# The last two groups turned on TensorE alone, and 4 of a second half's 16 moves handed from the sync queue to GpSimd

## The chip, the cores and the metric

One core of a Trainium2 chip runs the kernel. The metric is the device time of a whole execution, in microseconds (us), median over runs. The page and the trace come from one further execution taken with the hardware profiler.

## What is computed

One transformer block with adaptive layer norm, on x of 1 x 2048 x 128 in float32. Cut to what matters:

```python
h = _layernorm(x) * (1 + ca) + sa
q, k, v = split(einsum('bse,ehd->bshd', h, w_qkv), 3)        # 16 heads of 64
logits = einsum('bqhd,bkhd->bhqk', q, k) / sqrt(64)          # 2048 x 2048, causal
probs = softmax(where(mask, logits, neg))
x = x + ga * einsum('bshd,hde->bse', einsum('bhqk,bkhd->bqhd', probs, v), w_out)
h = _layernorm(x) * (1 + cb) + sb
expert = argmax(h @ Wr.T + br)                               # one of 8 for each token
x = x + gb * (relu(h @ W1[expert].T + b1[expert]) @ W2[expert].T + b2[expert])
```

## The kernel before

The 16 heads are taken as 8 pairs (PAIRS), and of each pair the 2048 queries as 8 groups of 256 (GROUPS). A group g has tiles_of(g) = 2g + 2 tiles of 128 keys. A group passes through these steps, each with the letter of its index in brackets (p pair, g group, r one of 4 rows of 128 queries of a head, j a key tile):

- score (L899, TensorE) puts scores into one of 4 PSUM banks; top (L1286, L1289, L1293, VectorE) copies them to `probs` in SBUF and takes the negated row maximum; exp (L1129, ScalarE) makes the exponentials in place, for one row r.
- The probabilities must be turned, keys to the partitions, before they can be multiplied by v. There are two ways. A *near* tile is turned on TensorE: turn (L912) is four 128 x 128 transposes into one of 3 PSUM banks, take (L1137 on ScalarE or L1322 on VectorE) copies them to one of 5 slots of `pT`. A *far* tile (j < far(g): 4 tiles of groups 3 and 4, 5 tiles of groups 5 to 7, none in groups 0 to 2) goes another way: shuffle (L1303, VectorE) transposes 32 x 32 blocks of a row r into `staged`, and moves (L650) carry the blocks to their partitions in `turned_far` by DMA.
- pv (L940, TensorE) multiplies a turned tile by v into one accumulating bank. Near tiles come first, far tiles last (pv_order, L66).
- sum, put and get (L1313, L699, L710) send reciprocal row sums through DRAM into a broadcast; norm (L1339), out (L953), add, and, in the last pair, back, resid, fresh, turn2, mod2, route, pick, rank, slots (L963 to L1415) finish 256 or 512 queries and find each token's place in a sorted list.

The moves. `staged` has two halves u: rows r = 0, 1 fill u = 0, rows r = 2, 3 fill u = 1. A half is 16 DMAs of 32 partitions each, in four batches a = 0 to 3 of four DMAs. The sync queue (SP) issues a = 0, 1 and GpSimd (POOL) a = 2, 3, of both halves; both queues run move_blocks (L641 to L651), which waits until the half is shuffled. Semaphores moved[u] (SP) and moved_soft[u] (POOL) each count 128 for a half. They are waited for in three places: by the far pv with j = 0 (L932, L933), for both halves; by the shuffle of the next group's rows r = 0 and r = 2 (L1301, L1302), for the same half, since `staged` is single; and by SP before the last stage (L731). There are 40 moves of a group (5 groups of 8 pairs).

SP also issues the puts (4 DMAs), the gets (2), the loads of each pair's weights, the blanks (L728), and in the last pair the 2 MB loads of W2 (L693) and W1 (L685) and b2 broadcast to all partitions (L686), each in a fixed place of its order. POOL also copies each chunk of k to its other 64 partitions (double, L795, two casts; the scores wait for it at L890) and, behind its last move, scatters the tokens (L803).

The order of every engine's work is made ahead, by class Plan (L101 to L413), a list scheduler on the host: it plays TensorE, ScalarE and VectorE with a duration per step (took, L318), a ready time per step (ready, L181), and moves that last 8 * ISSUE + LAND (5.2 + 4.2 us, move_at, L253). Each engine runs its list in that order with semaphore waits, so a change of a modelled time can reorder all three engines, SP (transfers, L280) and POOL (L159 to L162).

After the last pair: the experts' weights are transposed (wturn, L1036, L1039), the scattered tokens are read back in sorted tiles (L746), and 23 tiles go through the experts (L1055 to L1088).

Of the kernel before, what the change touches and what calls it, by code (L numbers as in the profile page):

```python
# [13 lines left out]
P = 128  # L14
# [4 lines left out]
PAIRS = 8  # L19
# [5 lines left out]
FAR_BUFS = 2  # L25
ISSUE = 650.0
LAND = 4200.0
# [33 lines left out]
def far(g):  # L61

    return FAR.get(g, 0)


def pv_order(g):  # L66

    return list(range(far(g), tiles_of(g))) + list(range(far(g)))
# [32 lines left out]
class Plan:  # L101
# [9 lines left out]
    def __init__(self):  # L111
        groups = [(p, g) for p in range(PAIRS) for g in range(GROUPS)]
        scores = [(p, g, r, c) for p, g in groups for r in range(4) for c in range(chunks(g))]
        turns = [(p, g, j) for p, g in groups for j in range(far(g), tiles_of(g))]
        pvs = [(p, g, j) for p, g in groups for j in pv_order(g)]
        self.moves = [(p, g) for p, g in groups if far(g)]
# [43 lines left out]
        for m, (p, g) in enumerate(self.moves):  # L160
            steps += [(self.move_at(m, u)[0] + 4 * ISSUE * i, "move", (p, g, u, 2 + i)) for u in range(2) for i in range(2)]
# [19 lines left out]
    def ready(self, kind, key):  # L181
# [8 lines left out]
        if kind == "pv":  # L190
            free = 0.0
            if key[2] == pv_order(g)[0] and p + g and min(groups_of(*self.part_of(p, g))) == g:
                free = at("norm", *self.part_of(*group_before(p, g)))
            return max(self.turned_at(key), at("value", p, key[2] // 4), free)
# [7 lines left out]
        if kind == "proj":  # L202

            last = (("score", p - 1, 2 * g + 1, 3, chunks(2 * g + 1) - 1), ("score", p - 1, GROUPS - 1, 3, g),
                    ("pv", p - 1, GROUPS - 1, max(range(4 * g, 4 * g + 4), key=pv_order(GROUPS - 1).index)))[key[2]]
            return max(self.ring_free(), at(*last) if p else 0.0)
        if kind == "top":
# [3 lines left out]
            if past and k0 < tiles_of(past[1]) * P:  # L211
                behind = at("shuffle", past[0], past[1], key[2]) if far(past[1]) else 0.0
                over = min((k0 + w) // P, tiles_of(past[1])) - 1
                if over >= far(past[1]):
# [9 lines left out]
        if kind == "norm":  # L224
            last = groups_of(p, g)[-1]
            i = p * CHUNKS + min(g, CHUNKS - 1) - 2
            return max([self.got(p, last), at("pv", p, last, pv_order(last)[-1])] +
# [9 lines left out]
        if kind == "wturn":  # L237
            free = max(at("pv", p, GROUPS - 1, pv_order(GROUPS - 1)[-1]),
# [14 lines left out]
    def move_at(self, m, u):  # L253

        if (m, u) not in self.moved:
            p, g = self.moves[m]
            begin = max(self.at("shuffle", p, g, 2 * u + r) for r in range(2))
            if m >= FAR_BUFS:
                q, f = self.moves[m - FAR_BUFS]
                begin = max(begin, self.at("pv", q, f, far(f) - 1))  # L260
            if u or m:
                begin = max(begin, self.move_at(m if u else m - 1, 1 - u)[0] + 8 * ISSUE)
            if begin >= NEVER:
                return NEVER, NEVER
            self.moved[m, u] = begin + HOP, begin + HOP + 8 * ISSUE + LAND
        return self.moved[m, u]

    def turned_at(self, key):

        p, g, j = key  # L270
        return self.move_at(self.move_no[p, g], 1)[1] if j < far(g) else self.at("take", *key)
# [8 lines left out]
    def transfers(self):  # L280
# [12 lines left out]
        for m, (p, g) in enumerate(self.moves):  # L293
            for u in range(2):
                for a in range(2):
# [4 lines left out]
                          self.at("shuffle", p, g - 1, 3) if far(g - 1) else 0.0) + HOP, "w2", (p,)))  # L300
# [17 lines left out]
    def took(self, kind, key, engine):  # L318
# [17 lines left out]
        if kind == "shuffle":  # L336
            return far(key[1]) * P / 0.96 + 100.0
# [43 lines left out]
    def choose_pe(self, now, soon):  # L381
# [11 lines left out]
        turn_at = place("turn", lambda k: (k[2] - far(k[1])) / float(tiles_of(k[1]) - far(k[1])))  # L393
# [23 lines left out]
def adaln_block(nc, x, w_qkv, w_out, Wr, br, W1, b1, W2, b2, c_in, wmod, out):  # L417
# [27 lines left out]
    with ExitStack() as ctx:  # L445
# [195 lines left out]
        def move_blocks(queue, key, landed):  # L641
# [4 lines left out]
            if m >= FAR_BUFS:  # L646
                q, f = plan.moves[m - FAR_BUFS]
                queue.wait_ge(pv_done, plan.order[q, f, far(f) - 1] + 1)
            for b in range(P // SQUARE):
                queue.dma_start(turned_far[b * SQUARE:(b + 1) * SQUARE, m % FAR_BUFS, u, a, 0:far(g), :],  # L650
                                staged[a * SQUARE:(a + 1) * SQUARE, u, b, 0:far(g), :]).then_inc(landed[u], 16)  # L651
# [4 lines left out]
        def _(sp):  # L656
# [21 lines left out]
            for s in plan.sp:  # L678
# [9 lines left out]
                elif s.kind == "w2":  # L688

                    sp.wait_ge(rows_turned, plan.number[p, GROUPS - 2, tiles_of(GROUPS - 2) - 1] + 1)  # L690
                    if far(GROUPS - 2):
# [38 lines left out]
            for u in range(2):  # L730
                sp.wait_ge(moved[u], 128 * len(plan.moves))  # L731
                sp.wait_ge(moved_soft[u], 128 * len(plan.moves))
# [107 lines left out]
        def _(pe):  # L840
# [26 lines left out]
            for s in plan.pe:  # L867
# [34 lines left out]
                elif s.kind == "turn":  # L902
# [3 lines left out]
                    if j == far(g):  # L906
# [8 lines left out]
                elif s.kind == "pv":  # L915
                    j = s.key[2]
                    first, last = pv_order(g)[0], pv_order(g)[-1]
# [10 lines left out]
                    if j < far(g):  # L928
# [251 lines left out]
        def _(dve):  # L1180
# [69 lines left out]
            for s in plan.dve:  # L1250
# [17 lines left out]
                elif s.kind == "top":  # L1268
# [6 lines left out]
                    if past and far(past[1]) and c == 0:  # L1275

                        dve.wait_ge(shuffled, 4 * plan.move_no[past] + r + 1)
                    if past and k0 < tiles_of(past[1]) * P and (r == 0 or (r == 2 and c == n - 1)):

                        over = min((k0 + w) // P, tiles_of(past[1])) - 1  # L1280
                        if over >= far(past[1]):
# [13 lines left out]
                elif s.kind == "shuffle":  # L1295
# [4 lines left out]
                    if m and h == 0:  # L1300
                        dve.wait_ge(moved[u], 128 * m)  # L1301
# [217 lines left out]
```

## Time and profile before

| | us |
|---|---|
| median of 3 runs | 979.15 |
| lowest, highest | 978.8, 984.84 |
| profiled execution, own time | 988.01 |
| its span, first to last instruction | 986.3 |
| TensorE busy in it | 913.3 |

The profiled execution is 8.86 us above the median of the runs. Engines: PE TensorE, PEld its weight loads, DVE VectorE, ACT ScalarE, POOL GpSimd; SPq the sync queue. Times of the trace are in us from the span's start. A pair lasts some 105 us.

### The profile page before, as it was taken

To read this page: it belongs to the slowest core of one execution; us is meant where nothing else is said; L and a number is where in the kernel's file an instruction comes from. 1 tells how busy PE (TensorE), PEld (TensorE's weight loads), DVE (VectorE), ACT (ScalarE), POOL (GpSimd) and SP (SyncE) were. 2 spreads that over 40 slices of the span, in tenths; PEclk is the share of its full clock that TensorE was granted. 3 is DMA by queue.
4 is the path that set the end of the run, shared out by engine and by line. 5 is a ranking of instruction groups with operands and counts; after the bars stand their busy time and mean duration, and the time that the engine had idled before them with its cause. 6 is when DMAs were issued, how large, how long until landed. Compare 5 with 4: busy or idle time off the path is not lost.

```text
span 986.3 us, 19842 instructions
## 1 busy us (share of the span) xinstructions
PE 913.3 (93%) x6115; PEld 674.7 (68%) x6115; DVE 761.9 (77%) x2426; ACT 633.8 (64%) x1158; POOL 422.6 (43%) x765
## 2 busy tenths in 40 slices
PE   4999999989998999899998999899989999995796
PEld 3776767667675767677676767676767666773796
DVE  6898869875997769785988599867978689971463
ACT  4876668656774768665865677577857566551574
POOL 0274515442364316542554236431745144445054
PEclk9899999999999999999999999999999999986898
DMA  2035312342144302531245214430343013372120
GB/s 81 12 91 133 100 38 64 104 125 66 29 111 109 92 23 79 136 99 47 56 106 131 66 30 113 111 95 22 88 118 87 20 47 84 87 226 69 31 67 18
DMA packets 107211, 79.13 MB, mean 80 GB/s; under 512 B 32935, under 2 KB 94163, under 8 KB 107106
## 3 DMA queue, kind: packets, MB, share of 16 engines
q1 hardware_dynamic: 85378, 51.57, 19.7%
q0 software_dynamic: 21728, 26.29, 10.2%
q8 instruction: 50, 0.82, 0.4%
q14 instruction: 55, 0.45, 0.2%
HBM read 18.21 MB, written 11.77 MB: 30 GB/s over the span
## 4 chain that ended last, share of the span: by engine, by line
PE 59%; SPq 16%; DVE 12%; issue 5%; DMA 4%; ACT 2%; another core or an unknown queue 1%; POOL 1%; POOLq 0%; DVEq 0%; ACTq 0%
PE ps L940 18%; PE ps L899 13%; SPq L650 12%; PE ps L912 12%; PE ps L878 4%; DVE probs L1286 4%; DMA turned_far<-staged 3%; PE ps L882 3%; PE ps L1064 2%; DVE probs L1289 2%; PE ps L1075 2%; PE ps L953 2%; SPq L710 2%; SPq L699 2%; DVE staged L1303 1%
## 5 line engine op out<-in xcount | busy, mean ns | idle before, releaser
L650 POOL DMA_DIRECT2D turned_far<-staged x640 | 313.1, 497 | 353.4 <-DVE staged L1303 340.4
L1129 ACT ACTIVATE probs<-probs,neg_max 128x128 f32<-128x128 f32 (+15 forms) x256 | 308.7, 1207 | 151.2 <-DVE neg_max L1293 148.6
L899 PE MATMUL ps<-k_both,q_both 128*128 128x512 f32 (+2 forms) x1280 | 344.1, 393 | 12.9 <-DVE probs L1286 7.7
L899 PEld LDWEIGHTS ps<-k_both,q_both 128*128 128x128 f32 x1280 | 208.7, 190 | 84.9 <-issue 30.5
L1286 DVE TENSOR_SCALAR_CACHE_REDUCE probs<-ps 128x512 f32<-128x512 f32 (+1 forms) x384 | 243.4, 662 | 5.0 <-PE ps L899 4.0
L1137 ACT COPY pT<-ps 128x512 f32<-128x512 f32 (+1 forms) x341 | 177.1, 557 | 94.8 <-PE ps L912 76.3
L912 PE MATMUL ps<-ident,probs 128*128 128x128 f32 x1440 | 203.8, 278 | 2.3 <-ACT probs L1129 1.4
L912 PEld LDWEIGHTS ps<-ident,probs 128*128 128x128 f32 x1440 | 172.4, 143 | 46.5 <-issue 23.3
L940 PE MATMUL ps<-pT,v_sb 128*64 128x256 f32 (+1 forms) x1568 | 179.1, 370 | 5.7 <-DVE pT L1322 3.8
L940 PEld LDWEIGHTS ps<-pT,v_sb 128*64 128x64 f32 x1568 | 104.4, 137 | 74.0 <-issue 19.1
L1303 DVE STREAM_TRANSPOSE staged<-probs 128x640 f32<-128x640 f32 (+1 forms) x160 | 122.0, 778 | 37.6 <-DMA turned_far<-staged 15.9
L1289 DVE CUSTOM_DVE_ANT_0 probs<-ps,causal 128x256 f32<-128x256 f32 (+3 forms) x256 | 130.2, 509 | 8.1 <-PE ps L899 7.8
L795 POOL CAST k_both<-k_both 64x1024 fp32r<-64x1024 f32 x64 | 66.4, 1037 | 148.2 <-DVE k_both L1265 145.6
L940 PE MATMUL ps<-turned_far,v_sb 128*64 128x256 f32 x736 | 93.0, 400 | 17.8 <-DMA turned_far<-staged 17.8
L940 PEld LDWEIGHTS ps<-turned_far,v_sb 128*64 128x64 f32 x736 | 56.1, 143 | 43.0 <-issue 24.3
L878 PE MATMUL ps<-hT,w_pair 128*128 128x512 f32 x128 | 63.4, 599 | 0.2 <-DVE q_both L1261 0.2
L1261 DVE SCALAR_TENSOR_TENSOR q_both<-ps,q_both 64x512 fp32r<-64x512 f32 x64 | 44.1, 689 | 20.9 <-ACT q_both L1115 19.7
L1322 DVE COPY pT<-ps 128x512 f32<-128x512 f32 (+1 forms) x51 | 31.5, 617 | 30.0 <-PE ps L912 15.1
L1339 DVE TENSOR_TENSOR oT<-ps,rinv_b 128x512 f32<-128x512 f32 (+1 forms) x33 | 22.1, 670 | 41.7 <-PE ps L940 40.7
L1129 ACT ACTIVATION_READ_ACCUMULATOR probs<-probs,neg_max 128x1 f32 x256 | 48.8, 190 | 0.0
L1265 DVE TENSOR_TENSOR k_both<-ps,k_both 64x512 fp32r<-64x512 f32 x64 | 44.1, 689 | 5.7 <-ACT k_both L1115 4.5
L1293 DVE TENSOR_REDUCE neg_max<-row_max 128x1 f32<-128x1 f32 (+3 forms) x256 | 39.8, 155 | 8.9
(147 smaller groups left out, 700.7 us busy)
## 6 DMA issues: line engine op xcount, KB each, us to landing
turned_far<-staged POOLq DMA_DIRECT2D x384, 40.0 KB, 2.5
turned_far<-staged SPq DMA_DIRECT2D x384, 40.0 KB, 2.0
x_sorted<-blank SPq DMA_DIRECT2D x19, 458.5 KB, 5.3
rinv_b<-spread_rows SPq DMA_DIRECT2D x128, 64.0 KB, 2.7
turned_far<-staged SPq DMA_DIRECT2D x256, 32.0 KB, 1.9
turned_far<-staged POOLq DMA_DIRECT2D x256, 32.0 KB, 1.8
spread_rows<-rinv_rows SPq DMA_DIRECT2D x256, 0.5 KB
probs<-in_L_ffn_W_dram SPq DMA_DIRECT2D x1, 2048.0 KB, 11.6
```

The costliest lines, as they stand in the source:

```text
L650: queue.dma_start(turned_far[b * SQUARE:(b + 1) * SQUARE, m % FAR_BUFS, u, a, 0:far(g), :], staged[a * SQUARE:(a + 1) * SQUARE, u, b, 0:fa ...
L795: nc.gpsimd.tensor_copy(k_split[h][own_half(1 - h), :, cols], k_split[h][own_half(h), :, cols]).then_inc(k_doubled[c], 1)
L878: pe.matmul(ps_ring[:, s.bank, :], w_pair[:, p % 2, j, :], hT[:, c * BANK:(c + 1) * BANK], start=True, stop=True).then_inc(bank_full[s.ban ...
L899: m = pe.matmul(ps_ring[:, s.bank, 0:w], q_split[r % 2][:, q0:q0 + P], k_split[r % 2][:, part, k0:k0 + w], start=(part == 0), stop=(part = ...
L912: m = pe.transpose(ps_turn[:, n % TURN_BANKS, P * r:P * r + P], probs[g % 2][:, r, j * P:j * P + P], ident[:])
L940: m = pe.matmul(ps_o[D * h:D * h + D, o_half + P * u0:o_half + QG], v_sb[:, j, D * h:D * h + D], of_head[:, h], start=(j == first), stop=( ...
L1129: act.activation(row, row, ACT.Exp, bias=neg_max[:, g, r:r + 1], accum_out=row_sum[:, g, r:r + 1]).then_inc(exp_done, 1)
L1137: act.copy(pT[:, n % PT_SLOTS, lo:BANK], ps_turn[:, n % TURN_BANKS, lo:BANK]).then_inc(turn_taken[n % TURN_BANKS], 1)
L1261: m = dve.scalar_tensor_tensor(out=q_split[h][own_half(1 - h), cols], in0=whole, scalar=Q_SCALE, in1=q_split[h][own_half(h), cols].bitcast ...
L1286: dve.tensor_scalar(row, ps_ring[:, bank, 0:w], 1.0, LOWEST, ALU.mult, ALU.max, accum_out=highest).then_inc(bank_free[bank], 1)
L1289: dve.tensor_tensor_reduce(row, ps_ring[:, bank, 0:w], causal[:, BANK - w:], 1.0, LOWEST, ALU.add, ALU.max, highest).then_inc(bank_free[ba ...
L1303: dve.transpose(staged[:, u, :, 0:far(g), h * SQUARE:(h + 1) * SQUARE], probs[g % 2][:, r, 0:far(g) * P].rearrange("p (j b i) -> p b j i", ...
```

## The change

Three things: the far tiles are dropped for the last two groups of the last pair (groups 6 and 7 of pair 7), so that all their tiles are turned on TensorE; of a second half (u = 1) SP issues only batch a = 0 and POOL a = 1, 2, 3, while a first half stays two and two; and the planner's times for a half become 8 * ISSUE = 5.2 us for u = 0 and 12 * SOFT_ISSUE = 6.0 us for u = 1. The functions far and pv_order take the pair too; the calls that only pass it on are left out.

```diff
+LAST_NEAR = 2
+HARD, SOFT = (128, 64), (128, 192)
 ISSUE = 650.0
+SOFT_ISSUE = 500.0
...
-def far(g):
-
-    return FAR.get(g, 0)
+def far(p, g):
+
+    return FAR.get(g, 0) if p * GROUPS + g < PAIRS * GROUPS - LAST_NEAR else 0
...
-            steps += [(self.move_at(m, u)[0] + 4 * ISSUE * i, "move", (p, g, u, 2 + i)) for u in range(2) for i in range(2)]
+            steps += [(self.move_at(m, u)[0] + 4 * SOFT_ISSUE * i, "move", (p, g, u, 2 - u + i)) for u in range(2) for i in range(2 + u)]
...
             if u or m:
-                begin = max(begin, self.move_at(m if u else m - 1, 1 - u)[0] + 8 * ISSUE)
+                begin = max(begin, self.move_at(m if u else m - 1, 1 - u)[0] + (12 * SOFT_ISSUE, 8 * ISSUE)[u])
...
-            self.moved[m, u] = begin + HOP, begin + HOP + 8 * ISSUE + LAND
+            self.moved[m, u] = begin + HOP, begin + HOP + (8 * ISSUE, 12 * SOFT_ISSUE)[u] + LAND
...
             for u in range(2):
-                for a in range(2):
+                for a in range(2 - u):
                     steps.append((self.move_at(m, u)[0] + 4 * ISSUE * a, "move", (p, g, u, a)))
...
                         if j == 0:
                             for u in range(2):
-                                pe.wait_ge(moved[u], 128 * m_no + 128)
-                                pe.wait_ge(moved_soft[u], 128 * m_no + 128)
+                                pe.wait_ge(moved[u], HARD[u] * (m_no + 1))
+                                pe.wait_ge(moved_soft[u], SOFT[u] * (m_no + 1))
...
                     if m and h == 0:
-                        dve.wait_ge(moved[u], 128 * m)
-                        dve.wait_ge(moved_soft[u], 128 * m)
+                        dve.wait_ge(moved[u], HARD[u] * m)
+                        dve.wait_ge(moved_soft[u], SOFT[u] * m)
```

## Rows read from the trace of the kernel before

**Rows 1.** Busy time by stretch: us, busy per engine, granted clock, DMA share, GB/s.

```profile
50.00:785.00 735.00, 707.91 (x4756) 509.92 (x4755) 592.10 (x1782) 497.27 (x869) 331.25 (x616) 1.00 0.32 83
785.00:889.40 104.40, 98.39 (x635) 72.40 (x634) 91.30 (x347) 60.52 (x95) 45.48 (x87) 0.95 0.39 110
889.40:909.60 20.20, 10.09 (x45) 5.85 (x46) 2.51 (x11) 1.42 (x3) 10.56 (x12) 0.61 0.20 56
...
313.00:317.00 4.00, 4.00 (x21) 2.41 (x18) 2.26 (x7) 0.00 (x0) 1.58 (x4) 0.57 0.28 74
```

**Rows 2.** Waits, 50 to 785 us: total us, times, longest.

```profile
PE ps L940 <- DMA turned_far<-staged: 17.5, 12, 3.5
PE ps L899 <- DVE probs L1286: 6.5, 7, 1.0
...
DVE staged L1303 <- DMA turned_far<-staged: 15.9, 9, 2.7
```

**Rows 3.** Timeline of SP, 296 to 316.5 us.

```profile
299.51 1.49 SPq L699 DMA_DIRECT2D spread_rows<-rinv_rows  x4
302.49 1.29 SPq L710 DMA_DIRECT2D rinv_b<-spread_rows  x2
...
304.52 11.37 SPq L650 DMA_DIRECT2D turned_far<-staged  x16
```

**Rows 4.** Timeline of POOL, 255 to 366 us.

```profile
269.47 2.15 POOL L795 CAST k_both<-k_both 64x1024 fp32r<-64x1024 f32 x2
...
298.92 3.91 POOL L650 DMA_DIRECT2D turned_far<-staged  x8 [6.44 <-DVE staged L1303]
```

**Rows 5.** Timelines of PE from 204 and 311 us, of DVE from 307 us.

```profile
204.08 4.07 PE L940 MATMUL ps<-turned_far,v_sb 128*64 128x256 f32 x20 [3.11 <-DMA turned_far<-staged]
...
312.63 0.84 DVE L1303 STREAM_TRANSPOSE staged<-probs 128x640 f32<-128x640 f32 x1 [3.10 <-issue]
...
312.80 4.00 PE L940 MATMUL ps<-turned_far,v_sb 128*64 128x256 f32 x20 [3.46 <-DMA turned_far<-staged]
```

**Rows 6.** The chain that ended last: pieces of TensorE at full clock.

```profile
335.84 1.92 PE ps L912 x16
...
419.86 2.37 PE ps L940 x20
```

**Rows 7.** Issues of line L650, 150 to 785 us: ns min/median/max.

```profile
L650 SPq DMA_DIRECT2D turned_far<-staged x480: 512/591/1766, 157.0 to 765.2; - x160
L650 POOL DMA_DIRECT2D turned_far<-staged x480: 496/496/505, 157.2 to 761.5; - x160
```

**Rows 8.** DMA issues, the page: KB each, us from issue to landing.

```profile
turned_far<-staged POOLq DMA_DIRECT2D x384, 40.0 KB, 2.5
turned_far<-staged SPq DMA_DIRECT2D x384, 40.0 KB, 2.0
```

**Rows 9.** Groups of instructions by form, whole span.

```profile
L1137 ACT COPY pT<-ps 128x512 f32<-128x512 f32 x291 | 160.1, 588 | 84.6 <-PE ps L912 74.3 <-remote 6.8 <-PE ps L940 1.9
...
L1303 DVE STREAM_TRANSPOSE staged<-probs 128x640 f32<-128x640 f32 x96 | 79.0, 834 | 37.6 <-DMA turned_far<-staged 15.9 <-ACT probs L1129 11.7 <-issue 9.7
```

**Rows 10.** Timeline of SP at the end of the last pair.

```profile
876.18 7.43 SPq L686 DMA_DIRECT2D experts<-in_L_ffn_b_dram  x1
...
891.63 2.47 SPq L650 DMA_DIRECT2D turned_far<-staged  x4
```

**Rows 11.** Timeline of all engines, 884 to 931 us.

```profile
888.18 1.04 PE L912 MATMUL ps<-ident,probs 128*128 128x128 f32 x8
...
894.15 0.56 ACT L1144 ACTIVATE hT<-ps,mod 128x256 f32<-128x256 f32 x1 [7.53 <-issue]
...
899.38 0.69 DVE L1322 COPY pT<-ps 128x512 f32<-128x512 f32 x1 [14.68 <-remote]
...
905.05 4.54 PE L940 MATMUL ps<-turned_far,v_sb 128*64 128x256 f32 x20
...
909.64 0.42 DVE L1339 TENSOR_TENSOR oT<-ps,rinv_b 128x256 f32<-128x256 f32 x1 [3.56 <-PE ps L940]
```

More of the change, by code:

```diff
@@ L113, in __init__ @@
         scores = [(p, g, r, c) for p, g in groups for r in range(4) for c in range(chunks(g))]
-        turns = [(p, g, j) for p, g in groups for j in range(far(g), tiles_of(g))]
-        pvs = [(p, g, j) for p, g in groups for j in pv_order(g)]
-        self.moves = [(p, g) for p, g in groups if far(g)]
+        turns = [(p, g, j) for p, g in groups for j in range(far(p, g), tiles_of(g))]
+        pvs = [(p, g, j) for p, g in groups for j in pv_order(p, g)]
+        self.moves = [(p, g) for p, g in groups if far(p, g)]
         shuffles = [(p, g, r) for p, g in self.moves for r in range(4)]
@@ L270, in turned_at @@
         p, g, j = key
[L271 removed]
+        return self.move_at(self.move_no[p, g], 1)[1] if j < far(p, g) else self.at("take", *key)
     def part_of(self, p, g):
@@ L392, in choose_pe @@
         score_at = place("score", lambda k: (k[2] * chunks(k[1]) + k[3]) / (4.0 * chunks(k[1])))
-        turn_at = place("turn", lambda k: (k[2] - far(k[1])) / float(tiles_of(k[1]) - far(k[1])))
+        turn_at = place("turn", lambda k: (k[2] - far(*k[:2])) / float(tiles_of(k[1]) - far(*k[:2])))
         waiting = 0
@@ L647, in move_blocks @@
                 q, f = plan.moves[m - FAR_BUFS]
-                queue.wait_ge(pv_done, plan.order[q, f, far(f) - 1] + 1)
+                queue.wait_ge(pv_done, plan.order[q, f, far(q, f) - 1] + 1)
             for b in range(P // SQUARE):
-                queue.dma_start(turned_far[b * SQUARE:(b + 1) * SQUARE, m % FAR_BUFS, u, a, 0:far(g), :],
-                                staged[a * SQUARE:(a + 1) * SQUARE, u, b, 0:far(g), :]).then_inc(landed[u], 16)
+                queue.dma_start(turned_far[b * SQUARE:(b + 1) * SQUARE, m % FAR_BUFS, u, a, 0:far(p, g), :],
+                                staged[a * SQUARE:(a + 1) * SQUARE, u, b, 0:far(p, g), :]).then_inc(landed[u], 16)
         block = ctx.enter_context(nc.Block())
@@ L730, in _ @@
             for u in range(2):
-                sp.wait_ge(moved[u], 128 * len(plan.moves))
-                sp.wait_ge(moved_soft[u], 128 * len(plan.moves))
+                sp.wait_ge(moved[u], HARD[u] * len(plan.moves))
+                sp.wait_ge(moved_soft[u], SOFT[u] * len(plan.moves))
             sp.wait_ge(chosen_known, 1)
@@ L916, in _ @@
                     j = s.key[2]
-                    first, last = pv_order(g)[0], pv_order(g)[-1]
+                    first, last = pv_order(p, g)[0], pv_order(p, g)[-1]
                     part = plan.part_of(p, g)
```

38 lines of the change are left out of this document (19 added, 19 removed).

## The prediction

> **What bounds the kernel now.** I read the stretches first. From 50 to 785 us, seven of the eight pairs, TensorE is busy 707.9 of 735.0 us [rows 1]: it is the bound, and what can be won there is its idle time, 27.1 us, and whatever makes its work slower. The waits say what ends that idle time: 17.5 us in 12 waits of the far pv for the moves' DMAs, 6.5 us in 7 waits of a score for VectorE; VectorE itself waits 15.9 us for the same DMAs before a shuffle [rows 2]. So the moves are late, and the question is which queue is late. The timelines around 300 us answer it [rows 3, 4, 5]. The second half of group 5 of pair 2 is shuffled at 298.6 (POOL starts at 298.92, 0.3 us behind it) and POOL has issued its 8 by 302.8. SP first puts (299.51), gets (302.49) and sends one blank, and starts its 8 of that half only at 304.52; in a row with the 8 of the next group's first half they take to 315.9. TensorE, idle from 309.34, gets its far tiles at 312.80, and VectorE's next shuffle starts at 312.63, behind an idle 3.10 [rows 5]. POOL's share had landed by about 305.3 (302.8 + 2.5 [rows 8]); SP was the last by 7 us. This recurs in each pair.
>
> A stall costs more than itself. Behind this one the granted clock is 0.57 of full for 4 us, that is, mostly the 1.2 GHz level [rows 1], and the 20 matmuls of the far tiles take 4.00 us [rows 5] against 2.37 us at full clock [rows 6]: 1.6 us more. Behind the other long stall (3.11 us) they take 4.07, so the two together cost about 3.3 us.
>
> The end of the attention is the second place. From 889.4 to 909.6 TensorE is busy 10.1 of 20.2 us at 0.61 of the clock [rows 1]. Two things lie on each other. SP's 7.43 us for the b2 issue push the last four moves to 891.63 [rows 10], so they can't have landed before 894.1 + 2.0 = 896.1 [rows 8]. But TensorE's far pv starts only at 905.05, behind a near tile whose turn ended at 889.2 and whose copy on VectorE began at 899.38, after a 14.68 us wait put down to "remote"; ScalarE's step at 894.15 has a 7.53 us wait put down to "issue" [rows 11]. For neither is there a releaser in the records.
>
> **The change part by part.**
>
> *Second half split 4 and 12.* SP loses 4 issues of each second half, 4 x 0.591 = 2.4 us; POOL gains 4 x 0.496 = 2.0 us [rows 7]. Worked out at the place above: SP's backlog ahead of it shrinks too, since the second half of group 4 was also 2.4 us shorter. SP then puts at about 298.8 (end of the shuffles and sum), gets behind the put's landing at 301.9, blanks to 303.8 and issues 4 moves to 306.2: landed at 308.2 with the 2.0 us [rows 8]. POOL: 298.9 + 12 x 0.489 (8 take 3.91 [rows 4]) = 304.8, landed at 307.3. The half is complete at 308.2 instead of 312.6, 4.4 us earlier and 1.1 us before TensorE asks (309.34). The 3.46 us stall goes, and VectorE's 3.10 us too. The other stalls are the same pattern and shorter, so all could go. Ceiling: 17.5 + 3.3 = 20.8 us, and some of the 6.5 us of waits for VectorE. Floor from this side: nothing, if TensorE then waits for VectorE or ScalarE at the same places. VectorE is busy 592.1 of 735 us and ScalarE 497.3 [rows 1], so neither is the bound, but both run short queues against a planner that is now rebuilt. I take 13, two thirds of the ceiling, nearer to it because the engines behind have 19% and 32% of idle time.
>
> *The planner's times.* A second half is now planned to land 0.8 us later, 6.0 + 4.2 = 10.2 us behind its shuffle. The real one took 14.0 us in the example (312.6 - 298.6) and would take 9.6. So far the plan was too hopeful by 4.5 us, and with the change it is about right; that is a second reason for the stalls to go. The price is a reordering nobody chose: from -5 to +5 us by the sizes of single waits in [rows 2] times a few; I take 0.
>
> *Groups 6 and 7 of pair 7 near.* Added on TensorE: 10 turns of 4 transposes, 16 take 1.92 or less [rows 6], so 0.44 to 0.48 each: 4.4 us, half of it before the last score, half behind it, on an engine that is the bound (98.4 of 104.4 us [rows 1]): all of it is on the path. The pv of a tile costs the same from `pT` as from `turned_far`. Added on ScalarE or VectorE: 10 takes at 0.588 or 0.690 us [rows 9, 11], 5.9 to 6.9 us, hidden in ScalarE's idle 44 of 104 us. Removed from VectorE: 8 shuffles at 0.834 us, 6.7 us [rows 9], in a stretch where it is busy 91.3 of 104.4 us; this may let scores through sooner, 0 to 2 us, I take 0 since TensorE is there busier still. Removed: 32 issues each on SP and POOL, so POOL can start its scatters 10 us earlier, which nothing waited for.
> What is won is the wait for the moves. In the profiled execution 20.2 us pass between 889.4 and norm at 909.64, with some 7 us of TensorE work at full clock in them (10.1 us of which most ran at half). Without moves 13 us of it go, less 4.4: 8.6 us. But the profiled execution lies 8.86 us above the median, and the only waits without a releaser are here. If the other runs don't have them, the stretch is 11.3 us long there, the work 7, and 4.3 - 4.4 = 0 is left. Both ends stay in the range (-9 to +1); I take -3, nearer to the runs that are measured, as the half clock level behind the wait is there too.
>
> The Trainium skill has a rule against the first part: "SBUF — State Buffer", section "SBUF: two separate sides", says that descriptors of GpSimd's DMAs are written through a port pair shared with VectorE, so that they starve while VectorE is in a two-port mode. What this kernel's rows show is the opposite case: POOL's issues took 496 ns, at most 505, in 480 records beside a VectorE busy for 81% of the time, while SP's ran from 512 to 1766 [rows 7]. By the rule the moved issues would be the dear ones; by the rows they are the cheap ones, and the sum above goes by the rows.
>
> **Sum.** Profiled execution: 988.0 - 13 - 8.6 = 966. Against the median: 979.15 - 13 - 3 = 963. I forecast 963.
>
> **The rivals.**
>
> *B. The wait changes its name.* TensorE finds its far tiles in time and waits instead for VectorE's copies or for the exponentials. For it: the 7 waits on VectorE of 1.0 us, just ahead of the stalls [rows 2]. Against it: VectorE loses its own 15.9 us of DMA waits at the same time. A third of the ceiling stays, 6 us, with nothing at the end: 973.
>
> *C. The end is wholly real.* The waits without a releaser belong to each run and go with the moves that crowd the queues. For it: one of the three runs took 984.84. Against it: the 8.86 us. Then 979.15 - 17 - 13 = 949.
>
> *D. Slower: POOL becomes late for k.* POOL's copies of k stand in one queue with the moves: casts at 269.47 between two halves [rows 4]. If the plan puts a 12-issue half ahead of a copy for which TensorE waits, each of up to two such copies a pair comes 2.0 us later: 2 x 7 x 2.0 = 28 us, from which 16 of gain come off: 991. It decides once more than 8 of the 14 copies lie on the path. Against it: no record of TensorE waiting for these casts, and POOL is busy 45% [rows 1].
>
> *E. The port.* By the skill's rule named above, and as a mechanism here: each moved issue waits for one VectorE copy of 0.690 us [rows 11]. A half then takes POOL 12 x (0.496 + 0.69) = 14.2 us and lands 16.7 us behind the shuffle, 2.7 us later than now; with 12 stalls longer by 2.7 us, 32 us, and the end's 3 off: 1008. Against it: the even 496 ns [rows 7].
>
> **How the numbers follow.** Chances: forecast 0.55 (range of its own 955 to 970), B 0.19, C 0.16, D 0.06, E 0.04. The range takes in B and C and most of their spread: 947 to 976. One per cent, about what a measurement of this kernel can tell from no change, is 9.8 us: faster means under 969.4. Faster: nearly all of the forecast's, all of C's and a little of B's, 0.72. Within 1%: the rest of B and of the forecast, 0.21. Slower: D and E less a part of D that ends near zero, 0.07.
>
> **What would show it.** Right: the far pv's waits for DMA fall from 17.5 us to under 4, VectorE's 15.9 likewise, TensorE's share in the seven pairs rises above 0.975, the dips of the clock behind the stalls near 204 and 313 us are gone, the half's last issue is POOL's, and between the last score and norm of the last part there is no move. A pair shortens by about 2 us. Wrong: TensorE's idle time is as long but ended by VectorE or ScalarE (B); waits of the scores on the casts (D); POOL's issues above 500 ns (E); a long wait without a releaser at the end again, which would leave the profiled execution well above its median.

## The result and the profile after

The changed kernel takes 935.97 us (median of 4 runs, 935.38 to 936.53), the kernel before 982.0 in the same comparison (4 runs, 978.8 to 985.66). The ratio is 0.953, 95% interval 0.9486 to 0.9574. The forecast was 963.0 with a range from 947 to 976: right in its sign, and 11 us too high even at its lower end. Two runs of the kernel before in the last group of experiments, of 995.12 and 996.52 us, fell in the chip's slower state and are left out below.

The two profiled executions differ by 52.7 us (spans 986.3 and 933.6), the medians by 46.0: the profiled execution before lay 6.0 above its median, the one after 0.6 below. The reciprocal of a group's row sums is one instruction a group, 64 in all, and cuts the span into comparable pieces. Of the kernel before (number of records, ns min/median/max, first and last start):

```profile
L1313 DVE RECIPROCAL rinv<-row_sum x64: 135/177/179, 33.3 to 876.9; 128x4 f32<-128x4 f32 x64
```

Of the kernel after:

```profile
L1316 DVE RECIPROCAL rinv<-row_sum x64: 165/178/180, 33.5 to 842.0; 128x4 f32<-128x4 f32 x64
```

A pair has 8 of them. With the start of the first one of pairs 1 and 7 from the timelines (the pairs count from 0), the difference falls apart like this:

| stretch | before | after | difference |
|---|---|---|---|
| to the first reciprocal of pair 1 | 122.7 | 116.1 | -6.6 |
| pairs 1 to 6, up to the first of pair 7 | 635.0 | 607.3 | -27.7 |
| pair 7, first to last reciprocal | 119.2 | 118.6 | -0.6 |
| behind the last reciprocal, to the end | 109.4 | 91.6 | -17.8 |

So 34 us came ahead of pair 7's first reciprocal, where the forecast had 13, and 18 at the end, where it had 3 (8.6 in the profiled execution).

**The pairs.** The same six pairs in the busy times by stretch (columns as in [rows 1]), before:

```profile
122.70:757.70 635.00, 610.20 (x4073) 437.96 (x4071) 513.25 (x1550) 431.04 (x753) 280.33 (x521) 0.99 0.32 82
```

and after, with the stretch that [rows 1] has first:

```profile
116.10:723.40 607.30, 603.66 (x4106) 437.27 (x4104) 506.17 (x1542) 435.51 (x768) 342.21 (x649) 1.00 0.34 87
...
50.00:785.00 735.00, 727.71 (x4935) 527.80 (x4933) 614.47 (x1893) 522.35 (x920) 413.89 (x784) 1.00 0.33 85
```

TensorE's idle time in the six pairs falls from 24.8 us (635.0 - 610.2) to 3.6, and its share of 50 to 785 us rises to 0.990. But its busy time falls too, by 6.5 us, with no less work in it (4106 matmul records for 4073). That is the part that no view of idle time shows. TensorE's waits from 50 to 785 us, after, and VectorE's for the moves:

```profile
PE ps L902 <- POOL k_both L798: 1.8, 1, 1.8
PE ps L902 <- DVE probs L1289: 1.2, 2, 0.7
PE ps L902 <- DVE q_both L1264: 1.0, 1, 1.0
PE ps L902 <- DVE accT L1353: 1.0, 6, 0.2
...
DVE staged L1306 <- DMA turned_far<-staged: 0.4, 1, 0.4
```

The far pv (now L943) no longer stands in the list, against 17.5 us in 12 waits [rows 2], and VectorE's shuffle (now L1306) has 0.4 us of waits for a DMA left of 15.9. Of the 6.5 us of "busy", 2.9 are the far pv: its 550 matmuls were busy 68.9 us in these pairs before and 66.0 after (mean 396 and 382 ns, the longest 643 and 431), which is what the half clock behind the stalls takes. The waits of TensorE's weight loads (PEld) shrank too. Pairs 1 to 6, before:

```profile
PEld ps L940 <- issue: 34.2, 66, 3.7
PEld ps L899 <- issue: 22.0, 78, 0.8
PEld ps L899 <- DVE probs L1286: 21.1, 48, 1.2
```

and after:

```profile
PEld ps L902 <- issue: 21.7, 77, 0.4
...
PEld ps L943 <- issue: 16.7, 72, 0.4
PEld ps L902 <- DVE probs L1289: 11.1, 37, 0.4
```

The longest is now 0.4 us where it was 3.7 and 1.2. Weight loads overlap the matmuls, so a short wait of theirs need not show as idle time; that the remaining 3.6 us of "busy" lay there is likely, but not shown.

The place of [rows 3 to 5], in the timelines of the kernel after:

```profile
287.11 0.84 DVE L1306 STREAM_TRANSPOSE staged<-probs 128x640 f32<-128x640 f32 x1
...
288.15 9.76 POOL L653 DMA_DIRECT2D turned_far<-staged  x20 [5.97 <-DVE staged L1306]
...
287.79 8.81 SPq L653 DMA_DIRECT2D turned_far<-staged  x12
...
299.09 2.38 PE L943 MATMUL ps<-turned_far,v_sb 128*64 128x256 f32 x20
```

The shuffle ends at 287.95; POOL puts its 12 and the next half's 8 in one row, SP has done its 4 and the next 8 by 296.60, 8.7 us behind the shuffle (before: 304.52 + 11.37, 17.3 us behind it, for 16 [rows 3]). The far pv starts at 299.09 behind no wait and at full speed: 2.38 us where it took 4.00 [rows 5].

Issues on POOL and landings, from the page, after:

```profile
L653 POOL DMA_DIRECT2D turned_far<-staged x760 | 371.5, 497 | 229.9 <-DVE staged L1306 200.9
...
turned_far<-staged POOLq DMA_DIRECT2D x440, 40.0 KB, 2.7
turned_far<-staged SPq DMA_DIRECT2D x264, 40.0 KB, 2.8
```

**The end.** The kernel before issues its scatters in one long row from GpSimd. First and twelfth of the row:

```profile
883.87 1.05 POOL L803 DMA_INDIRECT x_sorted<-x_sb,slot  x1 [0.30 <-issue]
...
897.86 0.95 POOL L803 DMA_INDIRECT x_sorted<-x_sb,slot  x1 [0.31 <-issue]
```

The two long waits without a releaser of [rows 11] lie beside exactly this row. In the kernel after, groups 6 and 7 have no moves, so GpSimd is free from 808.5 and scatters in rows of 4, 4, 4, 2 and 2, each as its slots come. The first of each of the first four rows, and norm of the last part:

```profile
808.82 1.05 POOL L806 DMA_INDIRECT x_sorted<-x_sb,slot  x1 [0.30 <-issue]
...
815.61 0.96 POOL L806 DMA_INDIRECT x_sorted<-x_sb,slot  x1 [1.94 <-DVE slot L1418]
...
841.92 0.95 POOL L806 DMA_INDIRECT x_sorted<-x_sb,slot  x1 [21.57 <-DVE slot L1418]
...
854.00 0.96 POOL L806 DMA_INDIRECT x_sorted<-x_sb,slot  x1 [7.33 <-DVE slot L1418]
...
857.45 0.42 DVE L1342 TENSOR_TENSOR oT<-ps,rinv_b 128x256 f32<-128x256 f32 x1 [1.62 <-PE ps L943]
```

A wait is put down to "remote" where the profile shows no releaser for it. The trace after has none at all between 785 and 930 us. That made the scatters the suspect for the end, and the experiments start from there.

### The profile page after: what moved, and what is told of

It is laid out like the page before. It is cut to its first block, busy times and chain, and to the rows that moved or that the text cites. A ratio compares the mean times of both kernels' runs of the same rounds, so it can differ in the third digit from the quotient of the medians.

```text
span 933.6 us, 19844 instructions
## 1 busy us (share of the span) xinstructions
PE 895.1 (96%) x6155; PEld 666.9 (71%) x6155; DVE 748.4 (80%) x2407; ACT 640.3 (69%) x1179; POOL 481.3 (52%) x885
## 3 DMA queue, kind: packets, MB, share of 16 engines
q1 hardware_dynamic: 76546, 44.55, 17.9%
## 4 chain that ended last, share of the span: by engine, by line
PE 84%; DVE 10%; issue 2%; ACT 1%; POOL 1%; DMA 1%; SPq 0%; POOLq 0%; DVEq 0%
PE ps L943 25%; PE ps L902 24%; PE ps L915 17%; PE ps L881 5%; PE ps L885 3%; DVE probs L1289 3%; PE ps L1067 2%; PE ps L956 2%; PE ps L1078 2%; DVE probs L1292 1%; POOL turned_far L653 1%; ACT probs L1132 1%; DVE accT L1353 1%; DVE oT L1342 1%; PE ps L1042 0%
## 5 line engine op out<-in xcount | busy, mean ns | idle before, releaser
L653 POOL DMA_DIRECT2D turned_far<-staged x760 | 371.5, 497 | 229.9 <-DVE staged L1306 200.9
L1140 ACT COPY pT<-ps 128x512 f32<-128x512 f32 (+1 forms) x362 | 186.0, 559 | 97.4 <-PE ps L915 79.6
L915 PEld LDWEIGHTS ps<-ident,probs 128*128 128x128 f32 x1480 | 176.1, 141 | 45.1 <-issue 25.7
L915 PE MATMUL ps<-ident,probs 128*128 128x128 f32 x1480 | 207.5, 274 | 0.6 <-ACT probs L1132 0.5
L943 PE MATMUL ps<-pT,v_sb 128*64 128x256 f32 (+1 forms) x1608 | 180.2, 367 | 0.5 <-ACT pT L1140 0.5
L943 PEld LDWEIGHTS ps<-pT,v_sb 128*64 128x64 f32 x1608 | 107.3, 136 | 64.2 <-issue 17.8
L1306 DVE STREAM_TRANSPOSE staged<-probs 128x640 f32<-128x640 f32 (+1 forms) x152 | 114.8, 774 | 3.4 <-ACT probs L1132 3.1
L943 PE MATMUL ps<-turned_far,v_sb 128*64 128x256 f32 x696 | 82.8, 383 | 0.0
L943 PEld LDWEIGHTS ps<-turned_far,v_sb 128*64 128x64 f32 x696 | 47.4, 137 | 23.8 <-issue 4.1
L1118 ACT ACTIVATE q_both<-ps 64x512 fp32r<-64x512 f32 x64 | 37.8, 591 | 10.7 <-PE ps L881 10.3
```

What stands on the lines that cost most here:

```text
L915: m = pe.transpose(ps_turn[:, n % TURN_BANKS, P * r:P * r + P], probs[g % 2][:, r, j * P:j * P + P], ident[:])
L943: m = pe.matmul(ps_o[D * h:D * h + D, o_half + P * u0:o_half + QG], v_sb[:, j, D * h:D * h + D], of_head[:, h], start=(j == first), stop=( ...
L1140: act.copy(pT[:, n % PT_SLOTS, lo:BANK], ps_turn[:, n % TURN_BANKS, lo:BANK]).then_inc(turn_taken[n % TURN_BANKS], 1)
L1306: dve.transpose(staged[:, u, :, 0:far(p, g), h * SQUARE:(h + 1) * SQUARE], probs[g % 2][:, r, 0:far(p, g) * P].rearrange("p (j b i) -> p b ...
```

## The experiments

Fourteen kernels ran, in four groups; those of a group share a chip and its runs of the kernel before. The kernel before had medians of 989.51 (e1 to e4), 985.05 (e5 to e8), 987.95 (e9, e12, e14, e15) and 987.07 us (e16, e17). The changed kernel ran in two of the groups, as e15 and, with pauses that do nothing there, as e8: 936.05 and 936.74, so that times of different groups can be set side by side to a few us.

| run | what it is | us | ratio [95%] |
|---|---|---|---|
| e1 | near tiles alone | 986.03 | 0.998 [0.995, 1.002] |
| e2 | split with its planner times | 959.46 | 0.971 [0.965, 0.978] |
| e3 | split alone, old plan | 957.82 | 0.970 [0.963, 0.976] |
| e4 | planner times alone | 976.15 | 0.988 [0.980, 0.996] |
| e5 | before, pauses between scatters | 981.29 | 0.993 [0.989, 0.997] |
| e6 | after, scatters late and in one row | 947.93 | 0.960 [0.954, 0.965] |
| e7 | e2, pauses | 952.42 | 0.965 [0.959, 0.971] |
| e8 | after, pauses | 936.74 | 0.949 [0.943, 0.954] |
| e9 | e2, first scatters early | 946.42 | 0.959 [0.952, 0.966] |
| e12 | after, three groups near | 942.51 | 0.956 [0.949, 0.963] |
| e14 | after, both halves 4 and 12 | 963.88 | 0.978 [0.971, 0.985] |
| e15 | after, again | 936.05 | 0.949 [0.943, 0.956] |
| e16 | after, second half 0 and 16 | 964.30 | 0.977 [0.972, 0.982] |
| e17 | after, one group near | 947.01 | 0.959 [0.954, 0.964] |

### The parts one by one

Near tiles alone (the changed kernel with the old issue and times):

```diff
-HARD, SOFT = (128, 64), (128, 192)
+HARD, SOFT = (128, 128), (128, 128)
```

(and the four places that follow from it: the batches of SP and POOL, two planner times.)

> Only the last two groups of the last pair lose their far tiles; moves and planner times stay as before. If the end is worth what the two profiles show behind the last sum (109.4 us against 91.6, 17.8 less, of which the profiled execution's excess of 6 us over its median is not in ordinary runs), the time falls by about 12 us to 970, and the seven pairs ahead keep their far waits of 17.5 us. If the end was only a one-off of one profiled execution: 979 to 982.

986.03 us, ratio 0.998: 3.5 us less than before and not told apart from nothing (interval -2 to 5). The forecast had 3. The far pv's waits in the pairs stay at 17.9 us. In the two traces the end behind the last reciprocal is 8.4 us shorter (101.0 against 109.4), and the stretch ahead of it 4.7 longer.

The split with its planner times, and no near group:

```diff
-LAST_NEAR = 2
+LAST_NEAR = 0
```

> The 4 and 12 split with the changed planner times, all far tiles kept. By the difference of the two profiles up to the last pair (34 us less) the time is about 948, and the stretch behind the last sum still takes 100 to 109 us. If the two parts help each other, it is above 955.

959.46 us, 30 less than before. The same with the planner left as it was, so that TensorE, ScalarE and VectorE do the same instructions in the same order as before, and only four issues of each second half change their queue:

```diff
-            self.moved[m, u] = begin + HOP, begin + HOP + (8 * ISSUE, 12 * SOFT_ISSUE)[u] + LAND
+            self.moved[m, u] = begin + HOP, begin + HOP + 8 * ISSUE + LAND
```

> The 4 and 12 split alone, with the planner's old times: TensorE, ScalarE and VectorE run the same instructions in the same order as before. Theory of the late queue: the moves land 3 to 4 us earlier, the far waits fall from 17.5 us to under 3, VectorE's 15.9 us go, and 30 of the 34 us come from this: 950. Theory of the order: the early landing is worth no more than the waits and the half clock behind them, 15 to 20 us: 964, and the rest needs the new order.

957.82 us: 31.7 less than before, with nothing reordered. Its pairs 1 to 6:

```profile
120.20:726.80 606.60, 603.26 (x4073) 431.69 (x4072) 512.38 (x1551) 430.90 (x753) 338.74 (x641) 1.00 0.33 86
```

They are 28.4 us shorter than before's 635.0: 21.5 of idle time (24.8 to 3.3) and 6.9 of busy time, for the same 4073 records. The far pv's waits for the moves from 50 to 785 us:

```profile
PE ps L943 <- DMA turned_far<-staged: 0.8, 1, 0.8
```

VectorE's before a shuffle are 3.4 us, of 15.9. So the late sync queue is shown to be the cause of the stalls, and its price is some 31 us (interval 24 to 37), not 13. The time lies between the two that were expected, 950 and 964, and the trace says why it isn't 950: in pair 7 the split alone loses, with 121.8 us from the first to the last reciprocal in e3 and 126.1 in e2 against 119.2 before, and the end behind it stays at 110 us.

The planner's new times with the old 8 and 8 (one line of the edit):

```diff
-                for a in range(2 - u):
+                for a in range(2):
```

> The changed planner times alone; SP and POOL issue 8 and 8 of each half, all far tiles kept, the same order of TensorE, ScalarE and VectorE as the run with the split alone. Theory of the late queue: the stalls stay, 976 to 984. Theory of the order: 962 to 970, since the planner now places far pv and shuffles 0.8 us later.

976.15 us, 13 less than before (interval 4 to 20): a plan that expects the half 0.8 us later puts other work ahead of the far pv, whose waits shrink to 0.4 us, and TensorE waits for VectorE's copies instead. The waits of 50 to 785 us:

```profile
PE ps L902 <- DVE probs L1289: 13.7, 6, 2.9
...
PE ps L943 <- DMA turned_far<-staged: 0.4, 1, 0.4
```

This is rival B, and it is real, but for the plan alone. Both cures attack the same stall, and together they don't add: the first reciprocal of pair 7 stands at 757.7 before, 743.9 with the plan, 726.8 with the split, 723.8 with both. On top of the split the plan wins 3 us up to there and loses 4.3 again in pair 7 (126.1 against 121.8), so that e2's median is 1.6 us above e3's: over the whole kernel it is worth nothing that these runs can tell.

### Long rows of scatters

The end of e2, where POOL issues 14 scatters in one row (first and last shown) behind the last moves:

```profile
857.46 1.05 POOL L806 DMA_INDIRECT x_sorted<-x_sb,slot  x1 [0.31 <-issue]
...
873.97 0.96 POOL L806 DMA_INDIRECT x_sorted<-x_sb,slot  x1 [0.30 <-issue]
...
868.09 0.66 PE L1039 MATMUL ps<-ident,w_rows 128*128 128x128 f32 x4
878.33 1.22 PE L956 MATMUL ps<-oT,wo_pair 128*128 128x256 f32 x2 [9.59 <-DVE oT L1342]
...
877.86 0.42 DVE L1342 TENSOR_TENSOR oT<-ps,rinv_b 128x256 f32<-128x256 f32 x1 [13.99 <-remote]
...
877.91 0.58 ACT L1154 COPY experts<-ps 128x512 f32<-128x512 f32 x1 [15.32 <-remote]
```

VectorE and ScalarE have both waited since 863.9 and 862.6, within the row, for results of TensorE, which ended its last pv at 868.16 and the transposes at 868.75. Both go on within 0.05 us of each other, 9.7 and 9.2 us behind those ends, when GpSimd's row and the TENSOR_TENSOR behind it are over. So the results lay ready for some 9 us; the rest of a wait of 13.99 or 15.32 us is TensorE's own work. TensorE stands 9.59 us.

To test it, pauses: behind the scatters of each part, GpSimd waits until they have landed.

```diff
                     pool.indirect_dma_start(x_sorted, bass.IndirectOffsetOnAxis(slot[:, t:t + 1], 0),
                                             x_sb[:, t, :], None).then_inc(scattered, 16)
+                pool.wait_ge(scattered, 16 * (first + n))
```

In the kernel before:

> The kernel before, with one wait more on GpSimd: behind each part's scatters (4, or 2) it waits until they have landed, so that the chain of 12 scatters in a row becomes 4, 4 and 4. Theory of the chain: the unexplained waits at the end (14.68 us on VectorE, 7.53 on ScalarE) belong to the long chain of scatters, as they lie in it in each profile with far tiles at the end; they go, and the time falls by 8 to 14 us, to 968 to 974 on a chip where before takes 982. Theory of the crowded queues (the 4.6 MB of weights with the last moves): nothing changes, 978 to 986.

981.29 us, 4 less (interval 3 to 10). The theory of the chain had expected 8 to 14, and the time lies in what the rival, the crowded queues, had expected (978 to 986), so that this run alone doesn't decide. In the traces the long waits shrink from 14.7 and 7.5 us to 5.3 and 4.0, and the end behind the last reciprocal is 8.3 us shorter (101.1). TensorE waits 8.40 us for the first sorted tile.

In e2 and in the changed kernel:

> The split with all far tiles kept, and the pauses between the scatters. If the end was lost to the chain alone, this comes near the changed kernel: 940 to 946, and the near tiles themselves are worth 3 to 8 us (the wait for the last moves, less 4.4 us of turns). If the moves at the end are the cost, it stays at 955 to 960.

> The changed kernel with the pauses. Its scatters already run as 8 with a gap of 1.94 us in the middle, and then 4, and no wait without a releaser shows: both theories say 934 to 938, no difference from the changed kernel. It ties this set to the changed kernel on one chip.

With e2, 952.42 us, 7 less, in another group (the ratios are 0.965 and 0.971, and their intervals overlap), and between the two that were expected, 946 and 955. The traces are clearer: no wait put down to "remote" is left, and the norm of the last part starts at 860.27, 17.6 us earlier. But the last scatter starts only 12.6 us earlier, since the pauses hold it up. It is what is late next. The first transpose of a sorted tile:

```profile
887.80 0.95 PE L1059 MATMUL ps<-ident,accT 128*128 128x128 f32 x2 [13.00 <-DVE accT L1475]
```

(a wait of 5.66 in the kernel after). In 14 of the 16 traces this transpose starts 7.0 to 7.2 us behind the start of the last scatter (e12 9.1, e16 9.3), and in those 14 the span ends 53 to 60 us after it. So a wait at the end costs about what it delays the last scatter. In the changed kernel, whose rows are short anyway, the same pauses do nothing: 936.74.

The reverse, in the changed kernel: GpSimd holds its first 12 scatters until the last score.

```diff
             pool.wait_ge(blanked, 16 * len(plan.blanks))
+            s_bank, s_use = plan.last_score
+            pool.wait_ge(bank_full[s_bank], s_use + 1)
             for i in range(len(parts_of(PAIRS - 1)) - 1):
                 scatter(i)
-            s_bank, s_use = plan.last_score
-            pool.wait_ge(bank_full[s_bank], s_use + 1)
```

> The changed kernel, its first 12 scatters held back until the last score, so that they run in a row beside the last turns and pv. No move is under way there. Theory of the chain: the waits without a releaser come back, 10 to 20 us more than the changed kernel, 946 to 956. Theory of the crowded queues by the moves: 936 to 940, as the scatters themselves are waited for only at the very end.

947.93 us, 12 more than after (11 more than e8 of the same group), with the same work on the other engines and no moves near. The waits are back:

```profile
838.11 1.05 POOL L806 DMA_INDIRECT x_sorted<-x_sb,slot  x1 [28.80 <-issue]
...
852.13 0.96 POOL L806 DMA_INDIRECT x_sorted<-x_sb,slot  x1 [0.30 <-issue]
...
846.65 0.59 ACT L1140 COPY pT<-ps 128x512 f32<-128x512 f32 x1 [4.69 <-remote]
...
853.72 0.69 DVE L1325 COPY pT<-ps 128x512 f32<-128x512 f32 x1 [9.44 <-remote]
...
855.18 0.59 ACT L1140 COPY pT<-ps 128x512 f32<-128x512 f32 x1 [4.38 <-remote]
```

The scatters of e2 that could go early, put early in GpSimd's order (parts 0 and 1, ahead of the last moves):

```diff
+        steps += [(self.at("slots", PAIRS - 1, i), "scatter", (i,)) for i in range(2)]
```

> The split with all far tiles kept, and GpSimd's first 8 scatters put into its order at the time when their places are known (one behind a move of group 3, one behind the first half of group 6), so that only 4 and 2 are left for the end. If the end gained by moving the scatters out of its way, and the near tiles only made room for that, this comes to within 5 us of the changed kernel. If the near tiles' own wait (last moves behind the b2 issue) matters as much, it stays 8 to 12 us above it. The 4 scatters delay the moves behind them by 5 us each, which may cost 1 to 3 us.

946.42 us: 13 of the 23 us that lie between e2 and the changed kernel, without one near tile, and 10 above the changed kernel, as was expected if the near tiles matter in themselves too. Here 6 scatters are left for a row, and the longest such waits are 6.5 and 6.2 us.

All runs together, with the longest row of scatters and the longest wait put down to "remote" between 785 and 930 us (the whole wait, not the lateness):

| longest row | runs and longest wait in us |
|---|---|
| 12 or 14 | before 14.7, e2 15.3, e3 17.0, e4 13.6, e6 9.4 |
| 6 or 8 | e1 4.3, e9 6.5, e16 2.6, e17 3.9 |
| 4 | e5 5.3; after, e7, e8, e12, e14, e15: none |

The one trace that doesn't fit is e5: TensorE's transposes end at 889.97 beside its first row of 4, and VectorE's copy starts at 892.12, 2.2 us later.

The rival of the crowded queues can be set against these traces. In e2 the DMA engines moved 42 GB/s on average from 858 to 884 us, and the long waits are there. In the kernel after the row of 4 from 841.92 lies in the 2 MB load of W2, 286 GB/s from 838 to 856 us, and nothing waits without a releaser. So crowding by weights or moves neither makes these waits by itself nor is needed for them. Late loading of the instructions isn't seen either: the profile shows their DMAs as queues of their own, and none moved a packet in e2 from 858 to 884 us.

### What the near tiles are worth, and the dose of the split

Three groups near instead of two (LAST_NEAR = 3), and one (LAST_NEAR = 1):

> The changed kernel with the last three groups near. Five more turns, 2.2 us, on TensorE, which is idle for under 1% there: 1 to 3 us above the changed kernel if nothing waits for group 5's moves or for the scatters; below it if GpSimd, free still earlier, matters.

> The changed kernel with only the last group (7) of the last pair turned on TensorE; group 6 goes by moves again. If the worth of the near tiles is that GpSimd is free for its scatters before the last score (theory 1), the 24 issues of group 6 on GpSimd (20 of 32: 10 us) come back in the place where 8 scatters stood: part of the 13 us of the early scatters goes: 940 to 945 us. If the worth is only that the last group's far pv doesn't wait (theory 2), this keeps it and saves 4 of the 10 added turns: 932 to 936 us. If each near group is worth the same (theory 3), half of the 23 us between 959.5 and 936: 947 us.

942.51 and 947.01 us: two is the best of the four (0, 1, 2, 3: 959.5, 947.0, 936, 942.5; on different chips, with before between 987 and 990). The third group adds 5 turns and frees nothing: no long wait was left. It costs 6.5 us against e15, where 1 to 3 were expected; the end behind the last reciprocal takes 102.9 us against 93.1, and why so much isn't shown. With one, the time is the one expected if each near group is worth the same (947), so the total decides nothing between the theories. In the trace the moves of group 6 return, the first two parts' scatters fall together into a row of 8 at 831 to 841, and the waits with them:

```profile
831.38 1.05 POOL L806 DMA_INDIRECT x_sorted<-x_sb,slot  x1 [0.30 <-issue]
...
838.60 0.69 DVE L1289 TENSOR_SCALAR_CACHE_REDUCE probs<-ps 128x512 f32<-128x512 f32 x1 [3.04 <-remote]
...
843.08 0.42 DVE L1342 TENSOR_TENSOR oT<-ps,rinv_b 128x256 f32<-128x256 f32 x1 [3.17 <-remote]
...
843.56 1.22 PE L956 MATMUL ps<-oT,wo_pair 128*128 128x256 f32 x2 [3.77 <-DVE oT L1342]
```

More on GpSimd: both halves 4 and 12, and the second half wholly on GpSimd. Both give it 24 of a group's 32 issues.

```diff
-HARD, SOFT = (128, 64), (128, 192)
+HARD, SOFT = (64, 64), (192, 192)
```

(e14; e16 has 128, 0 and 128, 256.)

> The changed kernel with 4 and 12 in both halves. The far waits are already gone (no far pv waits for a DMA in the profile after), so the theory of the late queue says no difference, within 2 us. If GpSimd is now near its limit (52% busy), first halves come late and waits for the moves or for the copies of k come back: 2 to 10 us more.

> The changed kernel with all 16 moves of a second half on GpSimd, none on the sync queue (first half 8 and 8). GpSimd then issues 24 of a group's 32, as many as in the run with 4 and 12 in both halves (964 us, pairs of 105.4 us against 100.9). Theory 1, the number that GpSimd issues in a group is what costs: about 964 us, and VectorE again waits for the moves before a shuffle, TensorE behind it. Theory 2, what cost there was GpSimd's share of the first half, which sits between two copies of k and the next half: about 936 us, within 3 us of the changed kernel, or up to 3 less if the sync queue was still late. Theory 3, between: a second half now takes GpSimd 16 x 0.49 = 7.8 us, 2 us more than the 5.9 of 12, and the half lands 2 us later in seven pairs at one or two places each: 940 to 950 us.

963.88 and 964.30 us, 28 more than after, each; of e14 at most 10 were expected. In e14 a pair takes 105.2 us, about as before the change (105.8), with before's pattern in another queue. In pair 2 GpSimd issues 8 of a first half's 12 from 259.57, copies a chunk of k, stands 2.36 us, for which the trace names no reason, and goes on with the last 4 at 268.03. VectorE's shuffle, which waits for them, starts at 271.61, behind 2.76 us, and TensorE waits behind it. From 50 to 785 us:

```profile
DVE staged L1306 <- DMA turned_far<-staged: 20.9, 7, 4.2
...
PE ps L902 <- DVE probs L1289: 14.8, 6, 3.4
```

e16 reaches the same time in another way: VectorE waits only 8.2 us for the moves, and TensorE's idle time is small (columns as in [rows 1], a whole pair, then the end behind the last reciprocal):

```profile
631.40:734.50 103.10, 101.43 (x686) 72.64 (x684) 86.72 (x263) 70.69 (x126) 66.52 (x128) 1.00 0.30 79
...
849.60:962.00 112.40, 89.09 (x710) 82.73 (x709) 52.36 (x188) 52.71 (x149) 33.52 (x38) 0.88 0.20 60
```

A pair is 2.3 us longer than the 100.8 of the kernel after, and the end (110.4 us) 19 longer, with more work left in it: 710 matmuls against 651 behind the last reciprocal, since the planner, told of 8 us for the half, ordered the turns otherwise. What of the 28 us is GpSimd's lateness and what the other plan wasn't separated in this run, so that the equal totals of e14 and e16 don't show that the number of issues is the cause.

The changed kernel again beside e9, e12 and e14:

> The changed kernel once more, as the reference of this set on the same chip: 935 to 938.

936.05 us, ratio 0.949. No run beat it.

## Why the prediction was wrong, and where it was right

**Right: what bounds and which queue is late.** TensorE bounds the pairs, the moves were late, and SP was the late queue [rows 2 to 5]: e3 moves four issues and nothing else, and the stalls go. The signs listed under what would show it came: far pv's waits for DMA 17.5 to 0, VectorE's 15.9 to 0.4, TensorE's share 0.990, and a granted clock of 1.00 near the old places (200 to 212 and 299 to 303 us). "A pair shortens by about 2 us" was short: 105.8 to 101.2 on average.

**Wrong: the size of the split, 13 for 31.** The failed step is "I take 13, two thirds of the ceiling", and the ceiling itself. The ceiling of 20.8 was put together from named waits. Of the 30.9 us by which e3's first reciprocal of pair 7 comes earlier, 16.7 are the far pv's waits (17.5 to 0.8) and 3.6 the far pv's busy time (68.9 to 65.3 in six pairs), as the ceiling had them. Two things were missing: TensorE's waits for VectorE, 5.8 us (6.5 to 0.7), which were listed as "some of" and went with the rest; and some 4 us more of TensorE's busy time, by subtraction (7.7 up to pair 7, less 3.6), whose place isn't shown. The discount of a third had no row behind it: the idle time of VectorE and ScalarE said that they could follow, and they did. The whole idle time of the bound, 27.1 us [rows 1], with the clock's 3.3 was the better ceiling, 30.4. That the run gave 31 is in part luck: 23 us of idle time went and 8 of busy time.

**Right: the planner, 0.** As an addition to the split it is worth nothing that the medians can tell (959.46 against 957.82), inside the bounds of -5 to +5. Alone it is worth 13, which the bounds, made from single waits, did not hold.

**Wrong: the end, 3 for 18.** Two steps failed. The first is the sentence "POOL can start its scatters 10 us earlier, which nothing waited for". The first scatter starts not 10 but 75 us earlier than before (808.82 for 883.87; 49 earlier than in e2), since the moves ahead of it had waited for their shuffles. And the row in which the scatters were issued lay beside the two waits without a releaser: e6 brings such waits in with the row, and e7 and e9, which break the row up or thin it, take them away or shorten them. Removing the moves broke the row up. What that is worth depends on the run: 4 us by e5, 7 by e7, 12 by e6, 13 of the near tiles' 23 by e9. Where the other 10 of these lie is only argued: the spans put 5.5 of them ahead of the last reciprocal (847.5 against 842.0) and 5.7 behind it, where e9 has moves, a row of 6 and its waits. The price set on the added turns wasn't measured apart; e12, one more group with 5 turns, costs 6.5 us.

The second is the weight given to the profiled execution, "the profiled execution lies 8.86 us above the median". From three runs it looked like an odd one. In the four groups the kernel before ran at medians from 985 to 990, single runs from 978 to 994, so 988.01 was an ordinary time, and the traces of e2, e3 and e4 have the long waits as well. The changed kernel's runs (those of e8 with them) lie from 935.2 to 937.3.

**Wrong: the parts don't add.** Near tiles alone brought 3.5, about the 3 of the forecast, and the split 30, but together they brought 46 to 52 in the three comparisons of the changed kernel, in place of 34. This is a third step that failed: the forecast added the terms one by one, and 12 us or more belong to neither part alone. The split by itself loses in pair 7 and keeps the long row at the end (e2, e3), and the near tiles take both away; without the split, e1 has the stalls still in its pairs and scatters in a row of 8.

**The rivals.** C (the end wholly real, 949) had the right sense at the end and named the wrong agent, the crowded queues; its 17 and 13 are both too small as well. B occurred only with the plan alone. D did not come about with this dose: TensorE has one wait of 1.8 us for a copy of k in the kernel after. With 24 issues a group (e14) GpSimd did become late, but for the moves and not for k. E is excluded: 497 ns a GpSimd issue over 760 records after, 496 before [rows 7]. The Trainium skill ("SBUF — State Buffer", section "SBUF: two separate sides") says that GpSimd can't write the descriptors of its DMAs while VectorE runs in a two-port mode; no run here shows its issues slowed so, though GpSimd now issued 19% more of these (760 for 640) beside a VectorE busy for 80% of the span. Whether VectorE was ever in such a mode the traces don't say.

## What to carry to other kernels

When a queue is late at a regular place, count the whole idle time of the bounding engine there as the prize, with the half clock, and discount it only for a reason that has a row. Busy time can shrink as well (6.9 us of it in six pairs here). A wait without a releaser is a finding: look at what every other engine does during it, here GpSimd's rows of indirect DMAs, before calling it a feature of one run. And test parts together as well as alone: the near tiles were worth 3.5 us by themselves and 23 behind the split, and a fifth more issues on the helper queue (912 for 760) gave the split's gain back.

## What the runs showed of the hardware that was not expected

While GpSimd issued a long unbroken row of indirect DMAs (one each 1.26 us), VectorE and ScalarE took up results of TensorE late: in e2 9.7 and 9.2 us behind the end of TensorE's work, in the kernel before 10.2 (the turn ended at 889.2, its copy started at 899.38). The whole waits were 9 to 17 us with rows of 12 and 14, 3 to 7 with rows of 6 and 8, and with rows of 4 there was none in six of seven traces. In e2 both engines went on together when the row and the instruction behind it were over. Only the link to the row is shown (e6 makes it, e7 takes it away); what in the chip holds the results back isn't, and e5, with rows of 4 and a wait of 5.3 us, stays unexplained.

Such a delay costs twice: behind the 9.59 us gap of e2 two matmuls of out took 1.22 us at a granted clock of 0.50 (the 1.2 GHz level), where the same two took 0.70 in the kernel after at 1.00.
